# A fused four-layer block on one core: top-3 gates of the later batches, with half the compares moved from VectorE to ScalarE

## The reference

```python
ss = jax.nn.sigmoid(x @ Ws).reshape(b, t, H, E)      # H = 8 heads, E = 5 experts
sd = jax.nn.sigmoid(x @ Wd).reshape(b, t, H, E)
ms = _topk_mask(ss, K)                               # K = 3
md = _topk_mask(sd, K)
ss_g = ss * ms
sd_g = sd * md
q5 = (x @ Wq).reshape(b, t, H, E, DH)                # DH = 64
kv = (x @ Wkv).reshape(b, t, 2, H, E, DH)
q = jnp.einsum('bthed,bthe->bhtd', q5, sd_g)         # k and v with ss_g
attn = jax.nn.softmax(jnp.einsum('bhid,bhjd->bhij', q * scale, k), axis=-1)
out = jnp.einsum('bhij,bhjd->bihd', attn, v)
o5 = jnp.einsum('bthd,dm->bthm', out, Wo).reshape(b, t, H, E, DIM)
return jnp.einsum('bthem,bthe->btm', o5, md)
```

## Time and profile before

| | |
|---|---|
| median of 3 runs | 1872.41 us |
| lowest and highest | 1870.97 and 1880.14 us |
| the profiled execution | 1878.52 us, of which the span of its instructions is 1876.6 us |
| TensorE's mean granted clock in it | 0.965 |
| the second layer's periods | first exponential at 284 us, 28.6 us a period where nothing is added |

### The profile page before, as it was taken

How to read it: one execution, slowest core, us unless ns; L and a number is a source line. 1 busy time by engine, 2 the same in 40 slices (tenths; PEclk the granted TensorE clock), 3 DMA queues, 4 the chain that set the end, 5 groups by cost and what they waited for, 6 DMA issues and landing times. The chain is left out here.

```text
span 1876.6 us, 26422 instructions
## 1 busy us (share of the span) xinstructions
PE 1695.8 (90%) x9454; PEld 867.2 (46%) x9454; DVE 1186.0 (63%) x1900; ACT 1216.8 (65%) x2359; POOL 892.4 (48%) x542
## 2 busy tenths in 40 slices
PE   7888569999999999999999999779999999898975
PEld 3434256555565555655555555324333333332354
DVE  6887987997779887698877667531414223120296
ACT  2122104766767476766677576668999999999833
POOL 3555305788776678756787677850000000000033
PEclk9999789999999999999999999979999999999988
DMA  3000032212112111211121110130221312201001
GB/s 86 0 11 1 1 117 81 86 44 86 54 44 60 39 54 44 65 40 54 38 65 54 44 54 23 57 124 23 68 91 42 116 45 69 83 31 37 1 12 36
DMA packets 38379, 97.65 MB, mean 52 GB/s; under 512 B 5008, under 2 KB 15968, under 8 KB 38112
## 3 DMA queue, kind: packets, MB, share of 16 engines
q1 hardware_dynamic: 38240, 95.86, 16.4%
HBM read 50.23 MB, written 28.84 MB: 42 GB/s over the span
## 5 line engine op out<-in xcount | busy, mean ns | idle before, releaser
L936 POOL TENSOR_TENSOR b_psum<-b_psum,b_probs 128x1024 f32<-128x1024 f32 x192 | 462.8, 2410 | 221.3 <-ACT b_probs L1078 215.0
L2369 ACT ACTIVATE c_probs<-banks 128x1024 f32<-128x1024 f32 x512 | 483.6, 1029 | 38.5 <-PE banks L2418 23.0
L1078 ACT ACTIVATE b_probs<-banks 128x1024 f32<-128x1024 f32 x256 | 255.4, 1020 | 230.0 <-PE banks L1218 229.3
L1183 PE MATMUL banks<-b_w,b_xh 128*128 128x480 f32 x1024 | 355.1, 399 | 34.2 <-issue 14.2
L1428 DVE TENSOR_TENSOR b_gated<-banks,b_g 128x480 f32<-128x480 f32 x512 | 310.2, 652 | 111.8 <-PE banks L1183 101.4
L1444 DVE TENSOR_REDUCE b_tok<-b_gated 128x192 f32<-128x960 f32 x256 | 281.3, 1137 | 0.5
L1047 ACT ACTIVATE b_share<-b_o,b_picked 128x64 f32<-128x64 f32 x1080 | 269.0, 340 | 1.7 <-DVE b_o L1469 1.7
L2432 PE MATMUL banks<-c_probs,c_vg 128*32 128x512 f32 x2048 | 251.0, 608 | 3.0 <-DVEq L2483 2.7
L1253 PE MATMUL banks<-b_probs,b_tok 128*64 128x512 f32 x1024 | 251.1, 611 | 2.6 <-ACT b_probs L1078 2.6
L1183 PEld LDWEIGHTS banks<-b_w,b_xh 128*128 128x128 f32 x1024 | 194.9, 190 | 117.8 <-issue 59.8
L1218 PE MATMUL banks<-b_qq,b_kk 64*128 64x512 f32 x1536 | 231.3, 424 | 5.4 <-DVE b_gated L1428 4.6
(11 more groups left out here) (248 smaller groups left out, 1807.6 us busy)
## 6 DMA issues: line engine op xcount, KB each, us to landing
b_w<-b_split_w SPq DMA_DIRECT2D x24, 960.0 KB, 4.7
b_kk<-b_kk SPq DMA_DIRECT2D x64, 256.0 KB, 3.6
c_heads<-c_split SPq DMA_DIRECT2D x24, 512.0 KB
c_keys<-c_heads SPq DMA_DIRECT2D x16, 512.0 KB, 3.7
c_queries<-c_heads SPq DMA_DIRECT2D x16, 512.0 KB, 4.7
b_split_w<-b_w SPq DMA_DIRECT2D x8, 960.0 KB, 6.1
b_raw_w<-in_L_ffn_W SPq DMA_DIRECT2D x8, 480.0 KB, 4.1
c_heads<-c_split SPq DMA_DIRECT2D x8, 384.0 KB
```

The lines of the kernel that those rows point to most:

```text
L936: nc.gpsimd.tensor_tensor(psum[:, par, :], prev, probs[:, i % 4, :], ALU.add).then_inc(psum_rdy, 1)
L1078: nc.scalar.activation(probs[:, i % 4, :], score_b[i % 2], ACT.Exp).then_inc(exp_rdy, 1)
L1183: last = nc.tensor.matmul(proj_b[u % WAYS][:, 0:HALF_W], a[:, x_of % 2, t * P:(t + 1) * P], w[:, par, part, j, :], start=(i == 0), stop=(i ...
L2369: nc.scalar.activation(probs[:, step % 4, c, :, :], unit_b[u % NU], ACT.Exp, scale=float(HD) ** -0.5).then_inc(exp_rdy, 1)
```

## The change

For the batches after the first, a generator of its own (`later_gate_parts`) makes the gates:

- The add of one is done by ScalarE, on all of `gate`, behind the split of x in round (1,0) (`add_one`).
- VectorE makes only the four `is_ge` compares, 1 to 4 experts wide, all in round (2,3). The other four entries are their complements, 1 - beats, which ScalarE writes in round (3,0) behind the copy of the queries (`mirror_beats`).
- The copy of the mask to `picked` is done by ScalarE in round (5,0) (`pick`), with a semaphore `picked_in` ahead of its use.
- The steps go one a round: reciprocals in (1,3), (2,0), (2,1), (2,2); the four compares in (2,3); sums in (3,2), (3,3), (4,0), (4,1); the compare with 3 in (4,2); the three laying operations together in (4,3). Rounds (3,0), (3,1) and all of head 5 have none.

Batch 0's gates stay as they were. The diff, without the parts that only rename:

```diff
-    GATE_STEPS = 2 + 4 + 2 * (E - 1) + 4 + 1 + 4
+    FIRST_STEPS = 2 + 4 + 2 * (E - 1) + 4 + 1 + 4
+    GATE_STEPS = 4 + (E - 1) + 4 + 1 + 3
+    GATE_ROUNDS = {(1, 3), (2, 0), (2, 1), (2, 2), (2, 3), (3, 2), (3, 3), (4, 0), (4, 1), (4, 2), (4, 3)}
+    MIRROR_ROUND, PICK_ROUND = (3, 0), (5, 0)
...
+    def add_one(self, act, b, gate_exp, ones):
+        act.wait_ge(gate_exp, 2 * b + 2)
+        self.nc.scalar.activation(self.gate[:, :, :], self.gate[:, :, :], ACT.Identity, bias=ones[:, 0:1]).then_inc(self.added, 1)
+
+    def mirror_beats(self, act, b, ones):
+        act.wait_ge(self.steps, self.steps_of(b) + 4 + self.E - 1)
+        for e in range(1, self.E):
+            self.nc.scalar.activation(self.beats[:, :, 0:e, e], self.beats[:, :, e, 0:e], ACT.Identity, bias=ones[:, 0:1], scale=-1.0).then_inc(self.mirrored, 1)
+
+    def pick(self, act, b):
+        act.wait_ge(self.steps, self.steps_of(b) + 4 + self.E - 1 + 4 + 1)
+        m = self.mask[:, :, :].rearrange("p (t s g) e -> p t s (g e)", t=NT, s=2)
+        self.nc.scalar.copy(self.picked[:, b % 2, :, :], m[:, :, 1, :]).then_inc(self.picked_in, 1)
+
+    def later_gate_parts(self, dve, b):
...
+        dve.wait_ge(self.added, b)
+        for t in range(0, NT, 2):
+            st.done(nc.vector.reciprocal(gb[:, t:t + 2, :], gb[:, t:t + 2, :]))
+            yield
+        st.settle()
+        g = gb.rearrange("p t (g e) -> p (t g) e", e=E)
+        for e in range(1, E):
+            st.done(nc.vector.tensor_tensor(beats[:, :, e, 0:e], g[:, :, 0:e], g[:, :, e:e + 1].broadcast_to([P, NT * NG, e]), ALU.is_ge))
+        yield
+        dve.wait_ge(self.mirrored, (E - 1) * b)
+        if b >= 2:
+            dve.wait_ge(self.picked_in, b - 1)
+        for c in range(0, NT * NG, NT * NG // 4):
+            some = slice(c, c + NT * NG // 4)
+            st.done(nc.vector.reduce_sum(mask[:, some, :], beats[:, some, :, :], AX.X))
+            yield
+        st.settle()
+        st.done(nc.vector.tensor_scalar(mask[:, :, :], mask[:, :, :], float(self.TOP), None, ALU.is_lt))
+        yield
+        st.settle()
...
+        for j in (1, 2):
+            st.done(nc.vector.tensor_tensor(laid[:, :, :, j, :], gs, by_head(m[:, :, 0, :]), ALU.mult))
+        st.done(nc.vector.scalar_tensor_tensor(laid[:, :, :, 0, :], gd, float(DH) ** -0.5, by_head(m[:, :, 1, :]), ALU.mult, ALU.mult))
+        st.settle()
+        assert st.n == self.GATE_STEPS, st.n
+        yield
...
                     if p == 0 and h == 1 and gates_next:
                         split_x(b + 1)
+                        front.add_one(act, b + 1, gate_exp, ones)
+                    if gates_next and (h, p) == front.MIRROR_ROUND:
+                        front.mirror_beats(act, b + 1, ones)
+                    if gates_next and (h, p) == front.PICK_ROUND:
+                        front.pick(act, b + 1)
...
-                    if gates_next and (2 <= h <= 5 or h == 1 and p == 3):
-                        next(waiting["gates"], None)
-                        if h < 4:
-                            next(waiting["gates"], None)
+                    if gates_next and (h, p) in front.GATE_ROUNDS:
+                        next(waiting["gates"])
```

More of the change, by code:

```diff
@@ L214, in __init__ @@
         self.clear, self.x_high, self.x_low, self.steps = map(sem, ("clear", "x_high", "x_low", "steps"))
+        self.added, self.mirrored, self.picked_in = map(sem, ("added", "mirrored", "picked_in"))
     def place(self, name, shape, dt=F32):
@@ L273, in split_low, with steps_of @@
             self.nc.vector.tensor_tensor(self.xl[:, b % 2, lo:hi], self.xT[:, lo:hi], self.xh[:, b % 2, lo:hi].bitcast(F32), ALU.subtract).then_inc(self.x_low, 1)
-    def gate_parts(self, dve, b, shares_done=None):
+    def steps_of(self, b):
+        return self.FIRST_STEPS + self.GATE_STEPS * (b - 1) if b else 0
+    def add_one(self, act, b, gate_exp, ones):
+        act.wait_ge(gate_exp, 2 * b + 2)
+        self.nc.scalar.activation(self.gate[:, :, :], self.gate[:, :, :], ACT.Identity, bias=ones[:, 0:1]).then_inc(self.added, 1)
@@ new lines, in later_gate_parts @@
+    def later_gate_parts(self, dve, b):
+        nc, gate, beats, mask = self.nc, self.gate, self.beats, self.mask
+        NH, E, NG, DH = self.NH, self.E, self.NG, self.DH
+        st = Steps(dve, self.steps, self.steps_of(b))
+        gb = gate[:, :, :]
+        dve.wait_ge(self.added, b)
[18 more added lines that the diff above has]
+        st.settle()
+        m = mask[:, :, :].rearrange("p (t s g) e -> p t s (g e)", t=NT, s=2)
+        by_head = lambda a: a.rearrange("p t (h e) -> p t h e", e=E)
+        gs, gd = by_head(gb[:, :, 0:NH * E]), by_head(gb[:, :, NH * E:])
+        laid = self.g15[:, b % 2, :, :, :, :]
+        for j in (1, 2):
[4 more added lines that the diff above has]
+        yield
@@ L276, in gate_parts @@
+    def gate_parts(self, dve):
+        b = 0
         nc, gate, beats, mask, picked = self.nc, self.gate, self.beats, self.mask, self.picked
         NH, E, NG, DH = self.NH, self.E, self.NG, self.DH
-        st = Steps(dve, self.steps, self.GATE_STEPS * b)
+        st = Steps(dve, self.steps)
         gb = gate[:, :, :]
@@ L302, in gate_parts @@
         m = mask[:, :, :].rearrange("p (t s g) e -> p t s (g e)", t=NT, s=2)
-        if shares_done is not None:
-            dve.wait_ge(*shares_done)
         st.done(nc.vector.tensor_copy(picked[:, b % 2, :, :], m[:, :, 1, :]))
@@ L315, in gate_parts @@
         st.settle()
-        assert st.n == self.GATE_STEPS, st.n
+        assert st.n == self.FIRST_STEPS, st.n
 def linear_into(nc, x_dram, out, ps, ident, I, place, signals, front):
@@ L717, in _ @@
                         dve.wait_ge(front.clear, 1)
-                        gates = front.gate_parts(dve, 0)
+                        gates = front.gate_parts(dve)
                     if j >= 6 and b == B - 1:
@@ L816, in switch_attention @@
         MOMENT_STEPS, NEWTON_STEPS = 2 * NT + 2, 14
-        GATE_STEPS = front.GATE_STEPS
         OUT_STEPS = 10
@@ L1010, in gate_exps @@
                 if not (isinstance(b, int) and b == 0):
-                    act.wait_ge(steps, GATE_STEPS * b)
+                    act.wait_ge(steps, front.steps_of(b))
                 front.exps(r, turn_b).then_inc(gate_exp, 1)
@@ L1041, in gated_share @@
                         act.wait_ge(zT_ps, ZT0 + OUT_STEPS * max(b - 1, 0))
+                    if b:
+                        act.wait_ge(front.picked_in, b)
                 if ts[0] % 4 == 0:
@@ L1413, in _ @@
             dve.sem_inc(o_rdy, O0)
-            def gate_parts(b):
-                dve.wait_ge(gate_exp, 2 * b + 2)
-                return front.gate_parts(dve, b, (share_rdy, SHARE0 + SHARES * NH * (b - 1)) if b >= 2 else None)
             def gate_part(n, b, h, t, j):
@@ L1497, in last_shares @@
                 dve.wait_ge(o_rdy, O0 + n + 1)
+                dve.wait_ge(front.picked_in, B - 1)
                 b, h = n // NH, n % NH
@@ L1525, in period @@
                 if gates_next and h == 1:
-                    waiting["gates"] = gate_parts(b + 1)
+                    waiting["gates"] = front.later_gate_parts(dve, b + 1)
                 if norm_last and h == 5:
@@ L1560, in period @@
                         lead.take(dve, k)
-                if gates_next and h == 5:
-                    for _ in waiting["gates"]:
-                        pass
             waiting = {}
@@ L1569, in _ @@
                 front.split_low(dve, 0)
-                for _ in gate_parts(0):
+                dve.wait_ge(gate_exp, 2)
+                for _ in front.gate_parts(dve):
                     pass
```

## The result

| | before | changed |
|---|---|---|
| median | 1872.49 us (12 runs) | 1881.72 us (12 runs) |
| lowest and highest | 1870.46 and 1880.36 | 1877.45 and 1886.71 |
| ratio to before | | 1.0043, 95% interval 1.0027 to 1.0059 |
| profiled execution | 1878.52, span 1876.6 | 1880.81, span 1879.0 |

The change made the kernel 9.2 us slower by the medians. The same two kernels were run once more later, on one chip: 1872.97 and 1885.57 us, ratio 1.0073 (1.0047 to 1.0099). So it is slower by 0.4 to 0.7%.

The account below looks back on a forecast made before the run. TensorE, busy 90% of the span, was taken as the bound. Terms -16.7 (gates' present cost), +13.4 (compares, batches 1 and 2), +10.2 (compares, batch 0), +4.5 (laying, batch 0) sum to +11.4 on 1872.4: 1884 us, range 1866 to 1890.

Parts of the forecast that it names:

- The mechanism: A stall traded for one a round earlier: four two-input compares in round (2,3) meet up to four GpSimd operations.
- The idle time: TensorE waiting for gate multiplies: 3.3 us in batches 1 and 2; batch 0 6.8 after (2,3), 2.8 after (4,3).
- the coin toss: Round (2,3), batches 1 and 2: VectorE taken to go before GpSimd at the third compare, turning on 0.02 us.
- The half clock: TensorE at about 1.2 GHz behind idle time: 3.4 us lost per stretch, 1.7 in batch 0 after (4,3).
- What goes: The gates' present cost in batches 0 to 2, 2.8 + 7.5 + 6.4 us, all freed for TensorE: -16.7.
- ScalarE covered: Four complements in round (3,0), at most 2.5 us, fit ScalarE's idle 3.14 us before the exponential: cost 0.
- The rival that priced them at 5.0: Complements cost twice the bound, 5.0 - 3.1 = 1.9 us in three batches: +5.7 on top, 1890; chance 0.05.
- The block: Round (2,3): all four compares pass before GpSimd gets a turn; -14.7, 1858 us, faster; chance 0.17.
- GpSimd first at the third compare: Round (2,3), batches 1 and 2: GpSimd precedes the third compare; 9.6 us each, +17.2, 1890; chance 0.12.
- the rival in which the stall stays about as long: Batch 0 finds one gap, no loss in (4,3), clock stays up in batches 1 and 2; -2.3, 1870; chance 0.28.
- the sign: Whole kernel: slower by more than 9.4 us, chance 0.50; faster by more, 0.20; within, 0.30.

## Why the prediction was right

Forecast were 1884 us (1866 to 1890) and slower by 0.6%; measured are 1881.7, and 1885.6 the second time. The mechanism is the one that I forecast. That the number came out so close is in part luck: the rise in the gates' cost, which the sum is about, was forecast at 11.4 us and is 3.5 in the first pair of traces (20.2 - 16.7) and 7.2 in the second (20.4 - 13.2). Point by point:

- **The idle time,** the heart of the sum: 3.3 us in batches 1 and 2, measured 2.98; 6.8 and 2.8 in batch 0, measured 6.10 and 2.71; 16.2 in all, measured 14.8. The round of batch 0 ended 1.0 us earlier than I had it: 0.3 of that at the first compare, since the split of weights had ended earlier, the rest because the three turns behind it took 2.4, 2.8 and 3.3 us where I had added 2.8, 2.9 and 3.5. At the third compare VectorE went first as I had taken it, in both batches and in both traces. It doesn't look like the coin toss that I took it for: in the second trace GpSimd's sum had been issued 0.05 us ahead of the compare (614.67 against 614.72) and still came behind it.
- **The half clock** was the mis-sized term. I charged 3.4 us behind each stretch, 1.7 behind the last, 11.9 in all; the trace shows 4.8. The step that failed is that I took the price from one execution. Idle time of 2.87 to 2.98 us is followed by 0, 3.4 or 6.9 us at half speed. Where the half clock began within a long idle stretch, part of it cost nothing.
- **What goes,** 16.7 us, was read from the same one execution, which stood 6 us above the kernel's median, with 6.9 us at half clock twice. The second trace has 13.2.
- **The rest.** The medians differ by 9.2 and 12.6 us, the gates' cost by 3.5 and 7.2. The 5 to 6 us between them I can't place, and they are what brings the sum so close. The profiled executions themselves differ by 2.3 and 16.7 us. Executions of one kernel differ by 10 us and more (1867.4 to 1880.6 in the repeat), much of it outside the rounds with gate steps: the periods began at 277.4 us in the second trace of before and at 284.0 in the first, and the period of head 6 of batch 3, which has no gate steps, took 28.5 us in the first trace of before and 31.7 in the other three of the two kernels. The periods began at 277.2 to 284.0 us in three traces of programs made from the kernel before and at 280.7 to 285.9 in nine made from the changed one; whether that is part of the rest is not shown.
- **ScalarE covered,** cost 0: right, but its working was wrong. I bounded four complements by 2.5 us and the cover by 3.1; they take 4.86. The cover was larger than the idle time that I read, because the exponentials of (3,1) may begin about 2 us late before TensorE waits for them. The rival that priced them at 5.0 had the size right and the stall wrong.
- **The rivals.** The block didn't happen: GpSimd got its turn between compares in each batch. Nor was GpSimd first at the third compare. Of the rival in which the stall stays about as long, one part came true: behind batch 1's 2.98 us the clock stayed up, in both traces. Batch 0 had no gap, and the sign was the forecast's.

## What to carry to other kernels

A side job that is cut into steps needs its steps placed by what they contend with, not by how long they are: the same four compares take 6.85 us in one round of batch 1 and 6.2 in two, 9.35 and 6.5 in batch 0, and TensorE waits 3 and 6 us for them in one round, less than 0.5 in two. Count the other engine's operations that are ready at that point, and compare with what the bound engine still has queued. Before work is moved off an engine, try moving it in time: two changed lines in the kernel before won, as far as medians can tell, what the whole change could win when its steps were well placed.

## What was not expected of the hardware

- A write of two-byte entries that stand ten bytes apart makes ScalarE nearly three times as slow: 2.00 us for 128x512, 1.00 for entries in groups of four, 0.73 in float32. The Trainium skill, ScalarE: Activation LUTs, section What ACT_TABLE_LOAD costs, gives one element a cycle for float32 and bf16 alike; with the fixed 280 ns that it gives for an instruction of this form, the 512 wide complement would take an estimated 0.7 us. The trace agrees for float32 (0.73) and not for bf16 in small pieces (1.00 and 2.00).
- Stretches of idle time that agree to 0.15 us (2.87 to 3.01) were followed by 0, 3.4 or 6.9 us at 1.2 GHz, in executions of the same program too.
- When a gate operation of two SBUF inputs ends and both the next such one and one of GpSimd's have been issued, GpSimd's goes first if it had been issued 0.13 us or more ahead: 47 of 47 in the second layer of all traces, up to four turns in a row. Where the two were issued within 0.05 us of each other VectorE's went first, 8 of 8. So a row of operations, each issued before the last has ended, does not keep the ports. The Trainium skill, SBUF — State Buffer, section Who interferes with whom, has whoever issues first get the shared ports for its whole instruction; the traces agree but for those 0.05 us, and show that it holds for each instruction anew. The same section says that an operation with at most one SBUF input does not contend with GpSimd; the sums of rows agree, all twelve of them at 0.98 us beside GpSimd's work.
